# The last group's query products: four terms summed by TensorE in a PSUM bank with the residual

## What is computed

```
kv  = einsum('bhil,bhjl->bijhl', k, v)            # k = v = ctx: a head is 8 of the 128 tokens, l one of the 256 features
y   = causal convolution of kv along l, by FFT, plus kv * D
out = einsum('bijhl,bhil->bjhl', y, q)            # q = x: sum over i of eight products
x   = layernorm(x + out)
```

## Time and profile before

| what | value |
|---|---|
| median of 3 runs | 582.54 us (582.50 to 587.96) |
| the profiled execution | 584.68 us |
| its span in the trace | 582.9 us |
| granted TensorE clock, mean of the span | 0.986 |
| busy: TensorE matmul, VectorE, ScalarE, GpSimd | 525.8, 389.8, 218.4, 239.2 us |
| DMA | 91.83 MB, mean 158 GB/s |

### The profile page before, as it was taken

The page is one execution under the profiler, slowest core; times in us unless marked ns, Lnnn a source line. Parts: engine busy times, 40 slices in busy tenths (PEclk is TensorE's granted clock), DMA queues, the critical chain, the costliest instruction groups (busy, mean ns, idle before and its releaser), DMA issues.

```text
span 582.9 us, 7010 instructions
## 1 busy us (share of the span) xinstructions
PE 525.8 (90%) x2241; PEld 321.5 (55%) x2241; DVE 389.8 (67%) x952; ACT 218.4 (37%) x441; POOL 239.2 (41%) x277
## 2 busy tenths in 40 slices
PE   7988999998899979999988999977969999997894
PEld 3334477644387744566754558743444555553673
DVE  3563236456958877997985986899875666662375
ACT  5482125721315654125572314510303333331142
POOL 4701002858501967600884901400026677742220
PEclk9999999999989999999999999998998999999998
DMA  7801990101000201010240010999947999996994
GB/s 276 309 1 53 416 401 32 38 0 36 0 2 1 91 1 36 1 37 0 92 148 2 0 36 2 303 272 289 274 151 223 326 332 321 310 297 200 413 414 169
DMA packets 39893, 91.83 MB, mean 158 GB/s; under 512 B 4512, under 2 KB 24384, under 8 KB 39728
## 3 DMA queue, kind: packets, MB, share of 16 engines
q1 hardware_dynamic: 34864, 75.45, 39.7%
q0 software_dynamic: 4992, 15.93, 8.6%
HBM read 67.02 MB, written 24.34 MB: 157 GB/s over the span
## 4 chain that ended last, share of the span: by engine, by line
PE 61%; DVE 20%; ACT 7%; DMA 5%; issue 4%; POOL 2%; SPq 1%; POOLq 0%; DVEq 0%; ACTq 0%
PE mb L745 19%; PE mb L1021 8%; PE kb L934 6%; DMA arena<-y_dram 4%; PE kb L1041 3%; PE kb L893 3%; PE kb L1039 2%; DVE arena L1101 2%; PE kb L773 2%; PE mb L751 2%; DVE cand L1161 2%; DVE arena L1087 2%; PE kb L764 2%; DVE first L1159 2%; DVE arena L1289 1%
## 5 line engine op out<-in xcount | busy, mean ns | idle before, releaser
L745 PE MATMUL mb<-arena 128*128 128x512 f32 x320 | 140.2, 594 | 7.7 <-DVE arena L1142 6.7
L430 POOL TENSOR_TENSOR arena<-arena 128x256 f32<-128x256 f32 (+7 forms) x128 | 76.1, 629 | 125.7 <-PE mb L797 125.7
L745 PEld LDWEIGHTS mb<-arena 128*128 128x128 f32 x320 | 60.1, 190 | 79.7 <-issue 70.1
L934 PE MATMUL kb<-arena 128*128 128x256 f32 x192 | 45.2, 391 | 4.9 <-DVE arena L1329 4.9
L649 ACT ACTIVATE arena<-mb,cols 128x512 f32<-128x512 f32 x24 | 16.5, 687 | 77.8 <-PE mb L745 77.7
L934 PEld LDWEIGHTS kb<-arena 128*128 128x128 f32 x192 | 36.5, 194 | 12.6 <-DVE arena L1329 7.6
L495 POOL DMA_INDIRECT y_dram<-shh,y_all x32 | 32.2, 1008 | 22.0 <-DVE shh L1469 14.2
L1021 PE MATMUL mb<-arena,x3T 128*64 128x352 f32 x224 | 39.3, 472 | 1.9 <-issue 1.9
L1329 DVE SCALAR_TENSOR_TENSOR arena<-mb,cols,arena 128x512 f32<-128x512 f32 x24 | 17.9, 744 | 28.3 <-PE mb L745 28.3
L751 PE MATMUL mb<-zeros,ident 128*128 128x512 f32 x60 | 30.9, 671 | 3.3 <-POOL ident L408 2.2
L1457 DVE TENSOR_TENSOR sgl<-mb,sgl 128x128 f32<-128x128 f32 x32 | 9.3, 292 | 34.9 <-ACT sgl L692 34.9
(11 more groups left out here) (239 smaller groups left out, 1061.2 us busy)
## 6 DMA issues: line engine op xcount, KB each, us to landing
arena<-in_w_experts_dram SPq DMA_DIRECT2D x28, 704.0 KB, 14.0
y_dram<-zeros SPq DMA_DIRECT2D x16, 768.0 KB, 11.1
arena<-y_dram SPq DMA_DIRECT2D x16, 768.0 KB, 13.2
arena<-in_w_experts_down_dram SPq DMA_DIRECT2D x56, 128.0 KB, 13.6
rows_dram<-rows POOLq DMA_DIRECT2D x4, 768.0 KB, 9.1
wextra<-in_w_experts_dram SPq DMA_DIRECT2D x4, 704.0 KB, 7.6
arena<-in_w_experts_down_dram SPq DMA_DIRECT2D x28, 96.0 KB, 14.3
arena<-in_x_dram SPq DMA_DIRECT2D x4, 512.0 KB, 3.5
```

The source lines that it names most:

```text
L430: last = e.tensor_tensor(v.kv[:, hb % 2, :, :, DOFF[d] * NB:DOFF[d] * NB + n], cx[:, :, :, 0:n], cx[:, :, :, d * NB:d * NB + n], ALU.mult)
L745: last = e.matmul(bank, w[:, c, n0:n0 + P], rhs[:, c, :], start=(c == 0), stop=(c == C - 1))
L934: last = e.matmul(kb[k][:, b * D:(b + 1) * D], v.mlp[:, j, t0:t0 + S], v.wdn[:, j, :], start=(j == 0), stop=(j == FJ - 1))
```

## The change

Only the last call of `step` (no head) changes; groups 0 to 2 keep `query_products` and the transposes.

- VectorE runs `last_products`, 12 steps in place of 15, on three buffers (`v.acc` and the two halves of `v.tmp`), with the diagonal's accumulator in `v.u` (`v.last_sum`). For d = 1, 2, 3 one buffer of the two that the products fill is added to the sum by VectorE, the other is left to TensorE as a term. Terms are ready after steps 3, 6 and 9; the fourth is the sum itself, after step 12 (`LAST_MADE`).
- TensorE first puts the residual `v.x2` into the two banks `tb` by a product with the identity, then, for each term, adds its transpose by eight float32 matmuls with the identity into the same banks. After each of the first three terms it raises `term_s`. The products `both(3, ...)` and `both(5, ...)` write the buffer of the first term and wait for its `term_s` of 1. `keep_clock(mb[0], 4)` goes.
- `shared_rows` stay before steps 2, 4 and 6, and `shared_sums` stands before step 10 in place of 12.
- The two residual additions (L1351) go; statistics and scaling read `tb` in PSUM instead of `v.u`.
- The normed rows are transposed into `mb[0]` and `mb[2]` instead of `tb`.

```diff
--- before.py
+++ after.py
@@ -180,6 +180,7 @@
         at[0] = at_left
 
         v.tmp = take(2 * CH * HD * NB).rearrange("p (t g n) -> p t g n", t=2, g=CH)
+        by_head = lambda t: t.rearrange("p (c h) n -> p c h n", c=C)
 
         def expert_weights(n, region):
             ring = []
@@ -197,6 +198,8 @@
         assert at[0] <= at_conv
         v.ring += expert_weights(WRING - 2 - W_X2 - W_CONV, arena)
         v.u = sb("u", [P, NB, D])
+        v.last_sum = v.u[:].rearrange("p b n -> p (b n)").rearrange("p (c h n) -> p c h n", c=C, h=HEADS)
+        v.last_terms = (by_head(v.tmp[:, 1]), by_head(v.tmp[:, 0]), by_head(v.tmp[:, 1]), v.last_sum)
         v.xg = [take(ROW) for _ in range(2)]
         for t in (v.x2, v.u):
             v.xg += [t[:].rearrange("p b n -> p (b n)")[:, k * ROW:(k + 1) * ROW] for k in range(2)]
@@ -392,6 +395,7 @@
 RDVE = 7
 QSTEPS = 2 * HD - 1
 QPART = 3
+LAST_MADE = (3, 6, 9, 12)
 PDVE = 17
 LAG = 4
 
@@ -659,7 +663,7 @@
                     if gs is not None:
                         wait(e, s["shu_done"], 2 * len(FSC) * (gs + 1))
                     e.activation(v.x3T[:, :, k * 2 * S:(k + 1) * 2 * S].rearrange("p c (b s) -> p b c s", b=2),
-                                 v.tb[k][:].rearrange("p (b c s) -> p b c s", b=2, c=C), ACT.Copy)\
+                                 (v.tb[k] if head else mb[2 * k])[:].rearrange("p (b c s) -> p b c s", b=2, c=C), ACT.Copy)\
                         .then_inc(s["x3T_s"], 1)
             if tail:
                 wait(e, s["logit_read"], gt + 1)
@@ -945,19 +949,32 @@
                 down([(0, 0)], False)
             if tail:
 
-                if not head:
+                if head:
+                    wait(e, s["qstep"], QSTEPS * gt + QSTEPS)
+                    wait(e, s["qpool"], QSTEPS * gt + QSTEPS)
+                    for k in range(2):
+                        for b in range(2):
+                            for c in range(C):
+                                last = e.transpose(tb[k][:, (b * C + c) * P:(b * C + c + 1) * P],
+                                                   v.acc[:, c].rearrange("p h (i b) -> p (h i) b", b=NB)[:, :, 2 * k + b],
+                                                   v.ident[:])
+                        last.then_inc(s["o_tr"], 1)
+                else:
                     wait(e, s["q_s"], 2 * gt + 2)
-                    keep_clock(mb[0], 4)
-                wait(e, s["qstep"], QSTEPS * gt + QSTEPS)
-                if head:
-                    wait(e, s["qpool"], QSTEPS * gt + QSTEPS)
-                for k in range(2):
-                    for b in range(2):
-                        for c in range(C):
-                            last = e.transpose(tb[k][:, (b * C + c) * P:(b * C + c + 1) * P],
-                                               v.acc[:, c].rearrange("p h (i b) -> p (h i) b", b=NB)[:, :, 2 * k + b],
-                                               v.ident[:])
-                    last.then_inc(s["o_tr"], 1)
+                    for k in range(2):
+                        e.matmul(tb[k][:], v.ident[:], v.x2[:, 2 * k:2 * k + 2, :], start=True, stop=False)
+                    for t, (term, made) in enumerate(zip(v.last_terms, LAST_MADE)):
+                        wait(e, s["qstep"], QSTEPS * gt + made)
+                        for k in range(2):
+                            for b in range(2):
+                                for c in range(C):
+                                    last = e.matmul(tb[k][:, (b * C + c) * P:(b * C + c + 1) * P],
+                                                    term[:, c].rearrange("p h (i b) -> p (h i) b", b=NB)[:, :, 2 * k + b],
+                                                    v.ident[:], start=False, stop=(t == len(LAST_MADE) - 1 and b == 1 and c == C - 1))
+                            if t == len(LAST_MADE) - 1:
+                                last.then_inc(s["o_tr"], 1)
+                        if t < len(LAST_MADE) - 1:
+                            last.then_inc(s["term_s"], 1)
             if head:
                 if gh + 1 < G:
                     features(gh + 1)
@@ -969,7 +986,7 @@
                     keep_clock(mb[1], 6)
                 wait(e, s["x3_s"], 4 * gt + 4)
                 for k in range(2):
-                    transposes(v.rows, k, "x3_tr")
+                    transposes(v.rows, k, "x3_tr", tb if head else (mb[0], mb[2]))
             if tail:
                 wait(e, s["x3T_s"], 2 * gt + 2)
                 for b in range(NB):
@@ -1105,6 +1122,49 @@
         parts += [lambda d=d: both(d, 1), lambda d=d: both(HD - d, 0), lambda: add(0, 0), lambda: add(1, 0)]
     parts += [middle, lambda: add(0, 0)]
     assert len(parts) == QSTEPS
+    return parts
+
+
+def last_products(e, v, steps):
+
+
+    WIDE = HD * NB
+    wide = lambda t: t.rearrange("p c h n -> p (c h) n")
+    y, q, total = wide(v.ycv), wide(v.q), wide(v.last_sum)
+    B = (wide(v.acc), v.tmp[:, 0], v.tmp[:, 1])
+
+    def runs(ap, at, step, n):
+        return bass.AP(ap.tensor, ap.offset + at, [list(ap.ap[0]), [step, 2], list(ap.ap[-2]), [1, n]])
+
+    def diagonal():
+        steps.did(e.tensor_tensor(total, q, y[:, :, 0:WIDE], ALU.mult))
+
+    def both(d, lo, other, taken):
+        n = (HD - d) * NB
+        yd = y[:, :, DOFF[d] * NB:DOFF[d] * NB + n]
+        wait(e, steps.sem, steps.base + steps.n)
+        wait(e, v.s["term_s"], taken)
+        steps.did(e.tensor_tensor(runs(B[lo], d * NB, B[other].offset - B[lo].offset - d * NB, n), runs(q, 0, d * NB, n),
+                                  runs(yd, 0, 0, n), ALU.mult))
+
+    def middle():
+        d = HD // 2
+        n = d * NB
+        yd = y[:, :, DOFF[d] * NB:DOFF[d] * NB + n]
+        wait(e, steps.sem, steps.base + steps.n)
+        steps.did(e.tensor_tensor(runs(B[0], n, -n, n), runs(q, 0, n, n), runs(yd, 0, 0, n), ALU.mult))
+
+    def add(k):
+        wait(e, steps.sem, steps.base + steps.n)
+        steps.did(e.tensor_tensor(total, total, B[k], ALU.add))
+
+    parts = [diagonal]
+    for d, lo, other, taken in ((1, 2, 1, 0), (2, 1, 0, 0), (3, 2, 0, 1)):
+        parts += [lambda d=d, lo=lo, other=other, taken=taken: both(d, lo, other, taken),
+                  lambda d=d, lo=lo, other=other, taken=taken: both(HD - d, other, lo, taken),
+                  lambda other=other: add(other)]
+    parts += [middle, lambda: add(0)]
+    assert len(parts) == LAST_MADE[-1]
     return parts
 
 
@@ -1313,7 +1373,7 @@
 
             if tail:
                 qsteps.begin(gt)
-                parts = query_products(e, v, qsteps, slice(0, CH_DVE if head else CH))
+                parts = query_products(e, v, qsteps, slice(0, CH_DVE)) if head else last_products(e, v, qsteps)
                 wait(e, s["conv_evac"], HEADS * gt + HEADS)
                 wait(e, s["q_s"], 2 * gt + 2)
             else:
@@ -1334,7 +1394,7 @@
                 for n, f in enumerate(parts):
                     if gs is not None and n in (2, 4, 6):
                         shared_rows(gs, n // 2 - 1)
-                    if gs is not None and n == 12:
+                    if gs is not None and n == 10:
                         shared_sums(gs)
                     f()
             if head and gh + 1 < G:
@@ -1344,15 +1404,19 @@
                 if head:
                     keep_first()
             if tail:
-                qsteps.end()
+                if head:
+                    qsteps.end()
                 rsteps.begin(gt)
                 for k in range(2):
                     wait(e, s["o_tr"], 2 * gt + k + 1)
-                    e.tensor_tensor(v.u[:, 2 * k:2 * k + 2, :], tb[k][:].rearrange("p (b n) -> p b n", b=2),
-                                    v.x2[:, 2 * k:2 * k + 2, :], ALU.add).then_inc(s["u_s"], 1)
-                wait(e, s["u_s"], 2 * gt + 2)
+                    if head:
+                        e.tensor_tensor(v.u[:, 2 * k:2 * k + 2, :], tb[k][:].rearrange("p (b n) -> p b n", b=2),
+                                        v.x2[:, 2 * k:2 * k + 2, :], ALU.add).then_inc(s["u_s"], 1)
+                if head:
+                    wait(e, s["u_s"], 2 * gt + 2)
+                summed = [v.u[:, b, :] if head else tb[b // 2][:, b % 2 * D:(b % 2 + 1) * D] for b in range(NB)]
                 for b in range(NB):
-                    last = e.bn_stats(v.bn[:, 1, b, :], v.u[:, b, :])
+                    last = e.bn_stats(v.bn[:, 1, b, :], summed[b])
                 n = rsteps.did(last)
                 wait_apart(e, v, rsteps.sem, n)
                 for b in range(NB):
@@ -1363,7 +1427,7 @@
                 wait(e, s["isB_s"], gt + 1)
                 wait(e, s["rows_out"], 16 * gt + 16)
                 for b in range(NB):
-                    e.tensor_scalar(v.rows[:, b, 0:D], v.u[:, b, :], v.mv[:, 1, b, 0:1], v.isB[:, b:b + 1],
+                    e.tensor_scalar(v.rows[:, b, 0:D], summed[b], v.mv[:, 1, b, 0:1], v.isB[:, b:b + 1],
                                     ALU.subtract, ALU.mult).then_inc(s["x3_s"], 1)
```

(2 more changed lines are left out.)

## The result

The changed kernel is slower: 1.013 times the kernel before, 95% interval 1.010 to 1.016. Its six runs have a median of 593.69 us (590.06 to 596.90). The kernel before, with three more runs taken beside them, has a median of 585.21. By the ratio the change costs about 7.6 us (5.9 to 9.2); the two medians lie 8.5 apart. The profiled execution took 596.90, with a span of 595.1.

What follows compares the result with a forecast made beforehand. VectorE's chain in the last group's tail was taken to bound the kernel. Stall +8.0, additions -3.75 and -1.27, PSUM reads +0.36, `keep_clock` and late last term +1.5 gave +4.8 us: median 587.3 us, range 584.2 to 589.6.

Steps and rivals of the forecast that it cites:

- Part 1: VectorE's work up to the second group of three: `shared_rows(gs, 2)` starts 0.54 us earlier, at 385.29.
- the place of the wait: VectorE stalls at `both(3, 2, 0, 1)`, from 387.14 to 395.15, until TensorE has taken the first term.
- Part 2: VectorE's new wait for the first term: 16 records at 0.12 us, 1.92 us a term, a stall of 8.0 us.
- rival B: Strided two-record loads in the terms overlap worse: over 1% slower, +6.4 us at pitch 0.17; chance 0.19.
- The cover I assumed: TensorE's term loads: line 957 hides about 90 of 209 ns; the same on 260 ns gives a pitch of 0.17.
- my outer bound: TensorE's term loads of 260 ns without any overlap: 4.2 us a term, +9.3 us in all.
- Part 3: Rest of VectorE's chain after the wait: 7.26 us instead of 8.51, rounds starting at 402.41, ending at 405.56.
- Part 4: TensorE's last term, after some 3.0 us idle: done at 404.7 at full clock, near 405.9 at half clock.
- Part 5: Norm and `keep_clock`: rows ready at 409.8 or 410.1; `keep_clock` ends at 409.7, or 411.3 with half clock.
- The sum: Shift of the last rows' transposes on TensorE: +3.3 us at full clock, +4.8 with half clock; +4.8 taken.
- The queues: SP queue's wait on `o_tr`: met at about 405.9, 4.7 us late, costed at nothing.

## Why the prediction was wrong, step by step

- **Part 1 (0.54 us earlier) and the place of the wait:** right. The order of TensorE's program put the first term behind the down products and the residual, and VectorE waited for it at the product that was named.
- **Part 2, the price of a term:** this is the step that failed. I took 0.12 us a record, from line 957; it is 0.234. What came true is rival B, at full clock (chance 0.19). The bound that I kept for the range, a load of 260 ns and a pitch of 0.17, came from adding the surcharge of the stride (209 - 140 = 69 ns, measured on transposes) to the load of a product (192). The load is 330: on a product the stride costs 138 ns, twice 69. The Trainium skill's load by columns alone ("TensorE: Matmul & The Clock Gate", LDWEIGHTS), 107 ns, does not hold here: loads of 128 columns took 192 to 330 ns for products, 140 and 209 for transposes. The cover I assumed, 90 ns, was about right: load and pitch differ by 78 to 97 ns in the six probes with data on the stationary side (192 and 112, 209 and 120, 330 and 233, for example). I had a row for a strided operand and one for two-record products but none for both together, and my outer bound, 0.26 a record, held it. Rival B priced that bound, but I ended the range at 0.17. Against 582.54, 1.013 is 590.1, and the range ended at 589.6.
- **Part 3:** right once the price is put in. The rounds start 24.06 us into the stage; the forecast, on the same clock, was 22.30, and 16 records at 0.114 more make 1.82.
- **Part 4, half clock:** wrong in the changed kernel, for the same reason. With records at twice the price TensorE had no 3.0 us of idle time before the last term (its weight loads paused for 0.22), and its clock stayed at 2.4 GHz. With contiguous weights the gap was there, 2.80 us, and so was half clock.
- **Part 5:** `keep_clock` held up the transposes, as forecast: its last record is followed at once by them. The rows were ready at 414.30 (412.40 + 1.90), so it held them up by about 0.5 us. The last term was not hidden under the rounds (statistics 1.0 us late). Scaling from PSUM costs 1.90 us for the four against 1.38 before, 0.5 where I had 0.28; the statistics cost nothing.
- **The sum:** rival B's rule, 0.32 us for each 0.01 of pitch, gives 3.3 + 11.4 x 0.32 = +6.95 at full clock. The stage measured +6.84. The structure of the sum was right and one term in it had the wrong size. That it comes within 0.11 us is in part luck: the 3.3 was counted along VectorE's path to the normed rows (409.8), and the measured end is set by the products of zeros, whose path the prediction happened to have at 409.7.
- **The queues:** SyncE's first preload behind `o_tr` went out at 409.91, 7.2 us later in the stage than before (forecast 4.7), and the next three 7.0, 5.6 and 3.5 later. The time from the last rows to the first expert product is the same. What their lateness costs in the expert phase itself, no run shows.

## What to carry to other kernels

Before work is moved to TensorE by float32 products over strided weights, look for a row of exactly that kind: type, two records and step together. A row that has only the step (a transpose) or only the type is half the price. Where a pipeline over two engines waits, add up the row of the engine that is waited for as well as the chain that waits: taking away the wait was worth 0.3 us here, halving the price of the row 2.1 us, and both together 8.0. Where a price is bounded by a guess on overlap, the outer bound belongs in the range.

## What the runs showed of the hardware that I had not expected

- A record of a float32 product costs twice as much from a step of 4 elements on, on either side: 0.233 us for strided weights, 0.227 for a strided moving side, 0.112 contiguous. At a step of 2 it is 0.118, at 3 0.173. A transpose at a step of 4 costs 0.120.
- At half clock the step costs nothing more: a load for a product takes 330 ns strided and 333 contiguous there, against 330 and 192 at full clock.
- VectorE pays for the same step: 1.99 us for an addition of 128x1024 float32 elements, 1.22 contiguous.
- Two calls of products of zeros, 0.86 us each and both in TensorE's gaps, made the kernel before 0.4% faster (0.9963, 0.9944 to 0.9982), though its profile had shown no half clock near them.
